# Attention stage of a two-layer kernel: query-weight splits all on GpSimd, softmax and mask steps reordered, result rows stored and reloaded batch by batch

## What is computed

```python
q = (layernorm(x2) @ Wq).reshape(b, t, 32, 128)      # 8 groups of 4 heads
k = (ctx @ Wk).reshape(b, t, 8, 128)
v = (ctx @ Wv).reshape(b, t, 8, 128)
q, k = rope(q), rope(k)
logits = 30 * tanh(0.08838834764831845 * einsum(q, k) / 30)
w = softmax(where(mask, logits, -1e30))
x3 = x2 + tanh(g) * (einsum(w, v).reshape(b, t, 4096) @ Wo)
```

## Time and profile before

| | us |
|---|---|
| median of 3 runs (3418.36 to 3420.48) | 3419.34 |
| profiled execution, as timed | 3422.15 |
| profiled execution, from first to last instruction | 3420.4 |
| mean granted PE clock, share of full speed | 0.968 |

### The profile page before, as it was taken

One profiled execution on the slowest core, in us unless ns is written; L12 is line 12 of the kernel. 1 busy time (PEld: TensorE's weight loads), 2 busy tenths in 40 slices (PEclk: granted clock), 3 DMA queues, 4 the chain that ended last, 5 costly groups with the idle time before them and its releaser, 6 DMA issues. The chain is left out here.

```text
span 3420.4 us, 41892 instructions
## 1 busy us (share of the span) xinstructions
PE 3114.4 (91%) x14675; PEld 2480.5 (73%) x14675; DVE 2179.1 (64%) x2665; ACT 1310.2 (38%) x2010; POOL 1822.8 (53%) x1233
## 2 busy tenths in 40 slices
PE   6999999999589999989999989999998999998699
PEld 4788788787467777767777767777776777776577
DVE  4777777775356665676566665666567656664575
ACT  4555555554233333433333333333343333332322
POOL 5454454443255556555655566556555565554343
PEclk8999999999689999999999999999999999999799
DMA  3011101110421212314121234121231312120321
GB/s 125 31 44 62 61 33 63 62 45 37 131 90 64 86 67 92 111 61 141 62 91 61 92 110 141 61 92 61 92 110 62 141 65 88 63 91 25 150 81 50
DMA packets 179312, 273.39 MB, mean 80 GB/s; under 512 B 8152, under 2 KB 108888, under 8 KB 179208
## 3 DMA queue, kind: packets, MB, share of 16 engines
q1 hardware_dynamic: 179208, 272.09, 23.4%
HBM read 238.51 MB, written 33.55 MB: 80 GB/s over the span
## 5 line engine op out<-in xcount | busy, mean ns | idle before, releaser
L1531 PE MATMUL gp_p<-g_xn_hi,g_wq_hi 128*128 128x512 f32 x1024 | 410.1, 400 | 103.5 <-DVE g_rot_b L1427 47.0
L1596 PE MATMUL gp_y<-g_wo_hi,g_at_hi 128*128 128x512 f32 x1024 | 406.7, 397 | 53.6 <-POOL g_wo_lo L1188 27.0
L1188 POOL TENSOR_TENSOR g_at_lo<-g_at_raw,g_at_hi 128x512 fp32r<-128x512 f32 x128 | 168.4, 1315 | 499.5 <-ACT g_at_hi L1277 499.5
L1469 DVE RECIPROCAL g_rot_b<-gp_sum 128x512 f32<-128x512 f32 x128 | 428.7, 3349 | 7.8 <-PE gp_sum L1579 7.6
L1596 PE MATMUL gp_y<-g_wo_hi,g_at_lo 128*128 128x512 f32 x1024 | 403.1, 394 | 0.0
L1596 PE MATMUL gp_y<-g_wo_lo,g_at_hi 128*128 128x512 f32 x1024 | 402.9, 393 | 0.0
L1531 PE MATMUL gp_p<-g_xn_lo,g_wq_hi 128*128 128x512 f32 x1024 | 400.2, 391 | 0.0
L1531 PE MATMUL gp_p<-g_xn_hi,g_wq_lo 128*128 128x512 f32 x1024 | 400.2, 391 | 0.0
L1446 DVE SCALAR_TENSOR_TENSOR g_res<-gp_y,g_tg,g_res 128x512 f32<-128x512 f32 x256 | 190.8, 746 | 238.1 <-PE gp_y L1596 221.6
L1188 POOL TENSOR_TENSOR g_prob_lo<-g_prob_raw,g_prob_hi 128x512 fp32r<-128x512 f32 x128 | 190.0, 1485 | 263.2 <-ACT g_prob_hi L1277 263.2
L1188 POOL TENSOR_TENSOR g_wo_lo<-g_wo_raw,g_wo_hi 128x1024 fp32r<-128x1024 f32 x128 | 315.8, 2468 | 18.7 <-ACT g_wo_hi L1277 18.7
(11 more groups left out here) (240 smaller groups left out, 7526.0 us busy)
## 6 DMA issues: line engine op xcount, KB each, us to landing
g_wq_raw<-in_L_Wq SPq DMA_DIRECT2D x64, 1024.0 KB, 7.5
g_wo_raw<-in_L_Wo SPq DMA_DIRECT2D x64, 1024.0 KB, 6.8
g_wkv_raw<-in_L_Wk SPq DMA_DIRECT2D x32, 512.0 KB, 4.6
g_wkv_raw<-in_L_Wv SPq DMA_DIRECT2D x32, 512.0 KB, 3.7
a_x<-in_x SPq DMA_DIRECT2D x16, 512.0 KB, 4.5
a_cc_f<-in_ctx SPq DMA_DIRECT2D x16, 512.0 KB, 5.0
a_cT<-in_ctxT SPq DMA_DIRECT2D x16, 512.0 KB, 3.7
x_after_layer<-a_x SPq DMA_DIRECT2D x16, 512.0 KB, 2.7
```

The costliest lines, as they stand in the source:

```text
L1188: return engine.tensor_tensor(view(buf["lo"]), view(buf["raw"]), view(buf["hi"]).bitcast(F32), ALU.subtract)
L1469: V.reciprocal(rsum[:, :], p_sum[:, :]).then_inc(rsum_done, 1)
L1531: mm = M(bank[:, :], w[a][:, i, cols], x[b][:, i, :], start=(i == 0 and t == 0), stop=(i == KT - 1 and t == 2))
L1596: mm = M(p_y[u % 2][:, :], at[p][:, h, bcols(b)], wo[r][:, h, half_ * BANK:(half_ + 1) * BANK], start=(h == 0 and t == 0), stop=(h == G - ...
```

## The change

1. All four `wq` quarters are split on POOL; DVE's `wq_split` goes. There is one semaphore `wq_lo` for the quarters, and PE waits for them one by one inside the first query projection. In an ordinary step the splits stand between the probability and attention splits of POOL's list (two behind the third probability split, two behind the fourth). In a group's last step `xn_split` stands behind the fourth probability split, and the four `wq` quarters behind `attn_split(2)`.
2. On ACT, `softmax(2)` stands ahead of the rounding of `wkv`, and `softmax(3)` between the first `wq` quarters. On DVE, `mask_probs(2)` and `mask_probs(3)` come right behind `normalise(0)` and `normalise(1)`, the key weights' split moves behind `add(4)`, the value weights' split behind the third rotation instead of the second. On PE, scores 2 comes ahead of values 0, and scores 3 behind out(3).
3. PE waits for the `wo` quarters one head at a time. The last step's `wo` goes into the `wq` buffers (`wo_last`), loaded as soon as the last query projection is done, and is split before the last attention split.
4. `res` is stored and loaded by batch: four semaphores `res_out`, three stores ahead of the `wo` load and the reloads behind it, the fourth store and reload around the load of the value weights. At the stage's end each batch is stored when its two additions are done.

```diff
+        wo_last = {t: wq[t][:, :, :].rearrange("p (h a) n -> p h (a n)", h=G) for t in ("raw", "hi", "lo")}
...
             def body(z):                                    # SP
...
+                if z.group_start:
+                    for b in range(NB - 1):
+                        store_res(z, b)
+                if z.last:
+                    sp.wait_ge(qk_proj, FIRST + n * NR + NR)
+                    load_halves("wo", wo_last, one(Wo_v, z.j))
                 sp.wait_ge(y_done, FIRST + n * NU)
-                load_halves("wo", wo, one(Wo_v, z.j))
+                if not z.last:
+                    load_halves("wo", wo, one(Wo_v, z.j))
                 if z.group_start:
-                    sp.wait_ge(y_added, FIRST + n * NU)
-                    sp.dma_start(one(res_dst, z.g - 1), res[:, :, :]).then_inc(res_out, 16)
+                    for b in range(NB - 1):
+                        reload(z, b)
+                    store_res(z, NB - 1)
...
+            for b in range(NB):
+                sp.wait_ge(y_added, FIRST + (NGRP * NKV - 1) * NU + 2 * b + 2)
+                sp.dma_start(x_out[(NGRP - 1) * NB + b], res[:, b, :]).then_inc(res_out[b], 16)
...
             xn_split(0)                                     # POOL
-            wq_split(0)
+            for m in range(4):
+                wq_split(0, m)
...
+                early = not z.last and not z.group_end
                 prob_split(0)
                 prob_split(1)
                 attn_split(0)
                 prob_split(2)
+                if early:
+                    wq_split(n + 1, 0)
+                    wq_split(n + 1, 1)
+                attn_split(1)
+                prob_split(3)
                 if z.group_end:
                     xn_split(z.g + 1)
-                attn_split(1)
-                prob_split(3)
+                if early:
+                    wq_split(n + 1, 2)
+                    wq_split(n + 1, 3)
                 attn_split(2)
+                if z.group_end:
+                    for m in range(4):
+                        wq_split(n + 1, m)
+                if z.last:
+                    for m in range(4):
+                        wo_split(n, m, wo_last)
+                attn_split(3)
...
                 softmax_hi(1)                               # ACT
+                early = not z.last and not z.group_end
+                softmax(2)
                 if not z.last:
                     wkv_round(2 * n + 3)
...
                 attn_hi(0)
-                softmax(2)
                 softmax_hi(2)
+                if early:
+                    quarters("wq", wq, n + 2, wq_hi, (0,))
+                softmax(3)
+                if early:
+                    quarters("wq", wq, n + 2, wq_hi, (1,))
                 attn_hi(1)
+                softmax_hi(3)
+                if early:
+                    quarters("wq", wq, n + 2, wq_hi, (2, 3))
...
                 normalise(0)                                # DVE
-                add(2)
                 mask_probs(2)
-                add(3)
-                if not z.last and not z.group_end:
-                    wkv_split(2 * n + 3)
+                add(2, 3)
                 normalise(1)
+                mask_probs(3)
                 add(4)
                 if z.group_end:
                     cx_split(z.g + 1)
+                if not z.last:
                     wkv_split(2 * n + 3)
-                mask_probs(3)
                 add(5)
                 normalise(2)
                 add(6, 7)
-                if not z.last:
-                    wq_split(n + 1)
                 normalise(3)
...
                     for i in range(NR):
                         rotate(n + 1, i)
-                        if i == 1:
+                        if i == 2:
                             wkv_split(2 * n + 4)
...
                 for i in range(KT):                         # PE, projection
+                    if fresh is not None and i % 2 == 0:
+                        pe.wait_ge(wq_lo, FIRST + 4 * fresh + i // 2 + 1)
...
                 for h in range(G):                          # PE, output
+                    if u == 0:
+                        pe.wait_ge(wo_lo, FIRST + n * 4 + h + 1)
...
                 out(1)                                      # PE, attend
+                scores(n, 2)
                 values(n, 0)
-                out(2)
-                scores(n, 2)
-                out(3)
+                out(2, 3)
+                scores(n, 3)
                 values(n, 1)
-                out(4)
-                scores(n, 3)
-                out(5)
+                out(4, 5)
                 values(n, 2)
```

More of the change, by code:

```diff
@@ L1057, in gqa_stage @@
         wkv_lo, wo_lo, cx_lo, xn_lo = sem("wkv_lo"), sem("wo_lo"), sem("cx_lo"), sem("xn_lo")
-        wq_lo = [sem(f"wq_lo{i}") for i in range(HALVES)]
-        res_in, res_out = sem("res_in"), sem("res_out")
+        wq_lo = sem("wq_lo")
+        res_in = sem("res_in")
+        res_out = [sem(f"res_out{b}") for b in range(NB)]
         qk_proj, v_proj, vT_out, v_turned = sem("qk_proj"), sem("v_proj"), sem("vT_out"), sem("v_turned")
@@ L1193, in _ @@
             nc.clear_and_free_semaphores(spent)
-            for done in (const_pool, xn_lo, wo_lo, rot_done, rot_lo, prob_lo, at_lo, wq_lo[0]):
+            for done in (const_pool, xn_lo, wo_lo, rot_done, rot_lo, prob_lo, at_lo, wq_lo):
                 pool.sem_inc(done, 1)
@@ L1206, in xn_split, with wq_split, wo_split @@
                         subtract_hi(nc.gpsimd, xn, part("xn", i, m)).then_inc(xn_lo, 1)
[L1208 to L1214, removed]
+            def wq_split(n, m):
+                pool.wait_ge(wq_hi, FIRST + n * 4 + m + 1)
+                subtract_hi(nc.gpsimd, wq, part("wq", m // 2, m % 2)).then_inc(wq_lo, 1)
+            def wo_split(n, m, buf):
                 pool.wait_ge(wo_hi, FIRST + n * 4 + m + 1)
-                subtract_hi(nc.gpsimd, wo, part("wo", m // 2, m % 2)).then_inc(wo_lo, 1)
+                subtract_hi(nc.gpsimd, buf, part("wo", m // 2, m % 2)).then_inc(wo_lo, 1)
             def rotated(n, i):
@@ L1346, in body @@
                 attn_hi(0)
-                softmax(2)
                 softmax_hi(2)
+                if early:
[3 more added lines that the diff above has]
+                    quarters("wq", wq, n + 2, wq_hi, (1,))
                 attn_hi(1)
+                softmax_hi(3)
+                if early:
+                    quarters("wq", wq, n + 2, wq_hi, (2, 3))
                 if z.group_end:
                     quarters("cx", cx, z.g + 2, cx_hi, range(4))
-                softmax(3)
-                softmax_hi(3)
                 attn_hi(2)
+                if z.group_end:
+                    quarters("wq", wq, n + 2, wq_hi, range(4))
+                if z.last:
+                    quarters("wo", wo_last, n + 1, wo_hi, range(4))
+                attn_hi(3)
                 if not z.last:
[L1356 to L1359, removed]
+                    for i in range(NR):
                         rot_round(n + 1, i)
@@ L1371, in _ @@
         def _(dve):
-            for done in (const_dve, cx_lo, wkv_lo, rot_mul, y_added, masked, rsum_done, attn_done, v_lo,
-                         wq_lo[1]):
+            for done in (const_dve, cx_lo, wkv_lo, rot_mul, y_added, masked, rsum_done, attn_done, v_lo):
                 dve.sem_inc(done, 1)
@@ L1399, in wkv_split @@
                 subtract_hi(V, wkv, lambda t: t[:, :, :]).then_inc(wkv_lo, 1)
-            def wq_split(n):
-                for m in range(2):
-                    dve.wait_ge(wq_hi, FIRST + n * 4 + m + 3)
-                    subtract_hi(V, wq, part("wq", 1, m)).then_inc(wq_lo[1], 1)
             def rotate(n, i):
@@ L1541, in project @@
                 pe.wait_ge(vT_out, FIRST + n)
-                for i in range(HALVES):
-                    pe.wait_ge(wq_lo[i], FIRST + 2 * n + 2)
                 for h in range(G):
@@ L1583, in values, with output @@
                 mm.then_inc(pv_done, 1)
-            def output(n, u):
+            def output(n, u, w):
                 b, half_ = u // 2, u % 2
-                if u == 0:
-                    pe.wait_ge(wo_lo, FIRST + (n + 1) * 4)
                 if half_ == 0:
@@ L1603, in out @@
                         for u in units:
-                            output(n - 1, u)
+                            output(n - 1, u, wo)
                 out(0)
@@ L1631, in _ @@
             for u in range(NU):
-                output(last, u)
+                output(last, u, wo_last)
 def sign_ffn_stage(nc, x_in, gate, signW, bias, gate_wT, in_scale3, out_scale3, x_out):
```

44 lines of the change are left out of this document (23 added, 21 removed).

## The result

The changed kernel took 3268.36 us in the median of 4 runs (3267.77 to 3270.21), beside 3419.91 for the kernel before on the same chip: the ratio is 0.9555, 95% interval 0.9538 to 0.9571. The forecast was 3277, range 3257 to 3310. The profiled execution was timed at 3270.21, its span is 3268.4.

A forecast was written before the change was run, and what follows sets the result against it. PE's stream, interrupted by waits, was taken as the bound; gains of 127 + 1 - 3 + 1 + 3 + 9.8 + 3.5 = 142 us from 3422.15 gave 3280, with the median 2.8 lower 3277, range 3257 to 3310.

The forecast's parts named there:

- Ordinary steps: 27 steps of the changed stage: 67.98 to 63.2 us, 4.7 taken as gained each (bounds 3.9 to 5.3), 127 in all.
- the hole of scores 2: PE's 0.7 us idle ahead of values 0, filled by three scores matmuls (0.68); some 0.25 stays per ordinary step.
- POOL's chain: POOL's rotation work from key addition to last q split, 26.8 us; ends at 63.4, PE wants it at 63.7.
- rival (b): POOL's rotation chain becomes the bound; one more meeting with DVE (1.1 us) per step, 3304 us; chance 0.17.
- Group ends: Three groups' last steps: stall behind `res` (8.9 us) grows by 3, projection stalls go; 1 us lost each, 3 in all.
- Step 0: First step, 66.77 us: normalisation chain stays, the projection's stalls (3.4) go; 3 us gained, bounds 1 and 6.
- Last step: PE paced by four early `wo` quarters, lower clock (references 0.93, 0.87); ends near 57.9, not 67.7: 9.8 us gained.
- Tail: Stores at the end: 512 KB remain instead of 2 MB, 2.7 us instead of 6.2; 3.5 gained, bounds 0 and 4.6.
- The mask: DVE's `mask_probs(3)` waits out POOL's second query quarter, ends at 19.35 instead of 18.4; values 3 stalls about 0.4 us.
- Rival (d): Slower: DVE's reciprocals also stand still behind POOL's quarters; steps of 70.2 us, 3463 us in all; chance 0.04.
- (a): Rival: the mask doesn't stand still behind POOL, 0.4 us less a step, 0.5 less per group end; 3263 us; chance 0.15.
- (c): Rival: POOL's list runs late, query quarters or fourth probability split come behind PE; half the gain, 3342 us; chance 0.09.

The follow-up runs named there:

- e3_quarter_later: The changed kernel with POOL's second query weight quarter moved behind its second attention split and fourth probability split, so the mask meets no POOL instruction: 3255.7 us.
- e1_dve_half: The changed kernel with the second half of the query weights split on DVE again, at its old place ahead of normalise(3), new orders kept: 3308.0 us.
- l1_last_back: The changed kernel with the last step's output weights loaded into their own buffer again and split behind the last attention split: 3279.8 us.
- r1_res_back: The changed kernel with `res` stored and loaded in one piece of 2 MB again instead of batch by batch: 3274.6 us.
- g3_group_nowait: The changed kernel with a group's last step laid anew, but POOL's query weight quarters not waiting for DVE's `wkv` split: 3264.2 us.
- g2_group_new: The changed kernel with a group's last step laid anew: `cx` splits behind normalise(2), `xn` splits spread out, POOL's `wq` quarters waiting for the `wkv` split: 3247.4 us.
- g1_xn_back: The changed kernel with `xn_split` back behind the third probability split, ahead of attn_split(1), in a group's last step alone: 3267.2 us.

## Why the prediction was right

- **Ordinary steps.** 63.2 was forecast, 63.10 came, so 4.86 was gained per step in the mean where I took 4.7. The sum by stalls holds: without one the step is 62.68 in `e3_quarter_later`, where idle times plus 0.28 for each had given 62.5, and the 0.25 that I left over in the hole of scores 2 covers the difference. The mask's wait was forecast to end at 19.35 and ended at 19.48 (1289.62 less 1270.14); the stall was 0.26 of idle for 0.4, and 0.42 in the step's length.
- **POOL's chain** ended at 1333.19, and the scores that need its last split started at 1333.59: it fitted by 0.4 in ordinary steps, where 0.3 was forecast. `e1_dve_half` shows that rival (b) was real: 2 us later on DVE put it on the path. At the group ends of the changed kernel it is on the path already. There the chain starts at 52.47 of step 7 (52.06 before), behind the four `wq` quarters and `attn_split(3)`, and with PE's other stalls gone PE now gets there first and waits at the turn of v that ends the step:
```profile
1475.24 0.66 PE L1587 MATMUL gp_pv<-g_ident,g_prob_raw 128*128 128x128 f32 x4 [1.28 <-ACT g_prob_raw L1328]
```
- **Group ends.** The stall of 12.3 and DVE's 15.3 for `cx` and `wkv` (forecast 15.4) came as laid out; `add(5)` ended at 35.8 for 36.1. The netting was off by 3 in all: I took 1 lost at each. Five smaller stalls went (two on the rotation, 1.3 together, 1.0 on `wq_lo`, 0.7 on the probabilities, 0.4 on `wo_lo`), 3.4 of idle time and, at 0.28 for each restart, 4.8. Against that stand the 3.4 by which the stall behind `res` grew and the new wait of 1.28, 4.7 (the restart behind that wait falls in the next step, which takes 63.56 for 63.10). Measured is 0.14 more for step 7. The forecast did not have the new wait, and that the terms cancel is luck.
- **Step 0** gained 4.5 for 3. Before, eight matmuls stand behind a stall, after four; their distances sum to 19.3 and 15.9, which is 3.4. That is the number that I had counted, but not all of its parts: I had the chain of normalisations unchanged, and its four waits grew from 13.2 to 13.9. The other 1.1 is in matmuls with no stall ahead of them that stand over 0.3 apart: 30 before and 21 after, at the lower clock. That I had left out.
- **Last step**: 9.8 and 9.8, with its four waits, of which 6.0 hang on the early load (`l1_last_back`). The clock was 0.91, between my two references.
- **Tail**: 2.5 for 3.5. SP's store wait fell by 4.0, but PE's first matmul of the next stage came only 2.1 earlier, as read in `r1_res_back`.
- **Not forecast**: 3.0 of the 152 are the unchanged first stage. Matmul for matmul, the kernel before falls behind by 1.4 in its first 110 us and by 1.6 near the stage's end; why isn't known, and it lies within the scatter of the twelve executions. Without it 149 stand against 142: 3 more from the ordinary steps (131.2 for 127 + 1), 3 from the group ends, 1.5 from step 0, less 1 from the tail.
- **The mask.** That it stands still was taken from the `wkv` split's case, and the earlier trace rows was called too short to tell. Those rows do tell: POOL's split ends at 1310.79 there and the mask at 1311.34, 0.55 behind it, just as in the changed kernel (1289.07 and 1289.62). In the trace of the kernel before 62 of the 128 masks start under a POOL split, and all end 0.54 to 0.56 behind it.
- **Rival (d)** is refuted by the reciprocal's 3.36 beside a `wq` quarter of 2.41. Of (a) only its time came near: 3263 is nearer to the measured 3268 than the forecast 3277 is, but only because the forecast was short in its other terms. (c) fell with the quarters' places: no wait on `wq_lo` is left in an ordinary step.

The Trainium skill (SBUF — State Buffer, section Who interferes with whom) says that a DVE instruction with two SBUF inputs contends with a GpSimd instruction that reads SBUF, and that the one that comes first has the shared ports for its whole length. By that rule the mask had to wait, and the trace agrees: 2.00 for 0.68, and 0.68 again when the quarter was moved. The reciprocal has one input, out of PSUM, and kept its length.

## What to carry to other kernels

Lay the lists of two engines that hold each other up beside each other, and count each meeting at the rest of the other's instruction; a wait on the engine that has time to spare can be worth more than the work it delays (16.7 us here). Two edits that free the same engine ahead of the same deadline don't add, two in different steps do: take apart by undoing as well as by doing alone. And when an ordinary step counts 27 times, 0.4 us in one row is worth more than a stall of 10 at one place.

## What the runs showed of the hardware

- When DVE and POOL both have splits queued, they take turns, one whole instruction each: a DVE split of 1.21 becomes 3.35, and four of POOL's, 9.42, become 13.20. Side by side both lists are through 15.5 us after DVE's first instruction (1427.58 to 1443.12 in `g3_group_nowait`), one behind the other 16.4 (1423.61 to 1439.97 in `g2_group_new`). So the overlap gains 0.8, and DVE's list, for which PE waits, is through 6.4 later.
- A mask of 0.68 that starts under a POOL instruction ends 0.55 behind it, whatever was left of that instruction: 2.00 in the changed kernel, 2.45 and 2.94 in `g2_group_new`, 1.53 in `g1_xn_back`, 0.73 in the earlier trace rows.
- Behind the stall of 12.3, in which PE had been idle, the first eleven distances are 0.59 and then 0.43, at a granted clock of 0.50 (the 1.2 GHz level), where 0.23 is usual at 1.00; behind them 0.23 is back. So a long stall costs some 2 us above its idle time: PE is busy 65.33 in that step and 62.84 in an ordinary one, with one list of matmuls. The window of the kernel after behind that stall, columns as in the earlier trace rows:
```profile
1432.17:1437.00 4.83, 4.83 (x11) 3.80 (x12) 4.56 (x3) 0.86 (x2) 0.15 (x1) 0.50 0.00 0
```
